# Another order of the same operations in the five instruction streams of a two-layer attention and convolution kernel

## The reference

```
y   = x + attention(group_norm(x))
out = y + conv(group_norm(y))
```

## Time and profile before

| what | value |
|---|---|
| median of 3 runs | 1963.32 us |
| profiled execution, time | 1962.26 us |
| profiled execution, span from first to last instruction | 1960.5 us |
| TensorE busy | 1861.5 us (95%) |
| VectorE busy | 1632.6 us (83%) |
| ScalarE busy | 1369.6 us (70%) |
| GpSimd busy | 1311.3 us (67%) |
| SyncE's DMA queue, share of the 16 DMA engines | 75.3% |
| mean granted TensorE clock | 0.989 |

### The profile page before, as it was taken

The page is one execution under the profiler, slowest core; times in us unless marked ns, Lnnn a source line. Parts: engine busy times, 40 slices in busy tenths (PEclk is TensorE's granted clock), DMA queues, the critical chain, the costliest instruction groups (busy, mean ns, idle before and its releaser), DMA issues.

```text
span 1960.5 us, 51383 instructions
## 1 busy us (share of the span) xinstructions
PE 1861.5 (95%) x21521; PEld 993.2 (51%) x21521; DVE 1632.6 (83%) x3108; ACT 1369.6 (70%) x1480; POOL 1311.3 (67%) x729
## 2 busy tenths in 40 slices
PE   3799999999999999999999999999999999999997
PEld 1455554555554555544555544555544555544552
DVE  6778888888888788888888888888888888888874
ACT  4677776776776777766777766777676777766761
POOL 6476767686666676767676767676667686667670
PEclk8989999999999999999999999999999999999999
DMA  6267877887877797877788878787877797877765
GB/s 130 46 139 157 178 165 155 169 176 160 171 164 161 150 180 157 178 164 159 162 181 152 178 162 157 163 181 150 180 160 161 157 182 156 177 165 157 156 145 145
DMA packets 349430, 313.01 MB, mean 160 GB/s; under 512 B 299152, under 2 KB 299920, under 8 KB 341008
## 3 DMA queue, kind: packets, MB, share of 16 engines
q1 hardware_dynamic: 346656, 305.75, 75.3%
q10 hardware_dynamic: 2224, 3.97, 0.8%
q0 software_dynamic: 320, 0.01, 0.0%
HBM read 68.10 MB, written 67.11 MB: 69 GB/s over the span
## 4 chain that ended last, share of the span: by engine, by line
PE 54%; SPq 21%; DVE 18%; DMA 4%; issue 2%; ACT 1%; POOL 0%; ACTq 0%; DVEq 0%; POOLq 0%
PE pair_ps L922 18%; PE pair_ps L904 8%; DVE km L1286 7%; SPq L334 6%; SPq L321 5%; PE pair_ps L913 5%; PE pair_ps L863 4%; SPq L333 4%; DVE u L1283 4%; DVE image L1338 4%; PE pair_ps L885 3%; PE bank_ps L814 3%; DMA replicas<-yg_lo 3%; PE pair_ps L823 3%; SPq L306 2%; SPq L327 2%
## 5 line engine op out<-in xcount | busy, mean ns | idle before, releaser
L922 PE MATMUL pair_ps<-replicas,w_rep 96*32 96x512 f16 x8192 | 490.3, 383 | 18.0 <-DMA replicas<-yg_lo 18.0
L489 POOL TENSOR_TENSOR u_lo<-u,u_hi 128x1024 f16<-128x1024 f32 x128 | 269.9, 2139 | 280.2 <-ACT u_hi L608 280.2
L492 POOL TENSOR_TENSOR exp_kT_lo<-exp_kT,exp_kT_hi 128x1024 f16<-128x1024 f32 x128 | 273.1, 2134 | 192.8 <-ACT exp_kT_hi L620 190.2
L922 PEld LDWEIGHTS pair_ps<-replicas,w_rep 96*32 96x32 f16 x8192 | 201.6, 96 | 279.8 <-issue 76.7
L495 POOL TENSOR_TENSOR u_lo<-exp_q,u_hi 128x1024 f16<-128x1024 f32 x128 | 270.4, 2142 | 25.7 <-ACT u_hi L626 25.2
L608 ACT ACTIVATE u_hi<-u 128x1024 f16<-128x1024 f32 x128 | 135.3, 1057 | 144.5 <-DVE u L1283 137.5
L1338 DVE SCALAR_TENSOR_TENSOR image<-pair_ps,image 128x512 f32<-128x512 f32 x256 | 175.5, 686 | 45.3 <-PE pair_ps L922 41.3
L626 ACT ACTIVATE u_hi<-exp_q 128x1024 f16<-128x1024 f32 x128 | 131.5, 1050 | 109.2 <-DVE exp_q L1325 109.0
L485 POOL TENSOR_SCALAR u<-image,st 128x1024 f32<-128x1024 f32 x128 | 179.3, 1409 | 29.4 <-DVE st L1222 29.4
L863 PE MATMUL pair_ps<-wqk_hi,u_hi 128*128 128x128 f16 x1024 | 181.5, 222 | 0.0
L1325 DVE TENSOR_TENSOR exp_q<-exp_q,pair_ps 128x1024 f32<-128x1024 f32 x128 | 152.9, 1216 | 32.8 <-PE pair_ps L823 29.8
(11 more groups left out here) (184 smaller groups left out, 4500.2 us busy)
## 6 DMA issues: line engine op xcount, KB each, us to landing
image<-in_x SPq DMA_DIRECT2D x256, 256.0 KB, 4.8
out<-image SPq DMA_DIRECT2D x502, 128.0 KB, 2.3
replicas<-yg_hi SPq DMA_DIRECT2D x252, 165.0 KB, 3.7
replicas<-yg_hi SPq DMA_DIRECT2D x252, 107.2 KB, 2.4
replicas<-yg_lo SPq DMA_DIRECT2D x126, 165.0 KB, 4.2
replicas<-yg_lo SPq DMA_DIRECT2D x126, 107.2 KB, 2.3
uT_hi<-u_hi SPq DMA_TRANSPOSE x128, 4.4
uT_lo<-u_lo SPq DMA_TRANSPOSE x128, 4.0
```

What stands on the lines that cost most here:

```text
L489: pool.tensor_tensor(px(UL, v), px(U, v), px(UH, v), ALU.subtract).then_inc(ul_ready, 1)
L492: pool.tensor_tensor(KL[:, v % 2], KT[:, v % 2], KH[:, v % 2], ALU.subtract).then_inc(kl_ready, 1)
L922: mm = pe.matmul(conv_ps[32 * r:32 * r + 32, j % 2], w_rep[0:32 * SLOTS, tap, r], rep[:, j * ROWS + dy:(j + 1) * ROWS + dy, dx:dx + SIDE], ...
```

## The change

No operation is added or taken away and none changes its size. Only the place in the stream, the PSUM tile of some, and the waits are changed:

- `inv_norm` 2 and 3, `normalise` 0 to 3, `rough_k` 0, `max_k` 0, `high_u` 0, `conv_dense` 6, `conv_ring` 5 and 6 and `finish` 5 and 6 move from the beginning of a step to the end of the step before.
- On VectorE `y_moments` goes between `row_k` and `max_q` 0, `y_seed` and `y_scale` between `max_q` 1 and 2, `low_y` 0 before `rows_q`, all `x_stats` behind `rows_q`; `keep_turned` goes behind two `soften`.
- On TensorE `context` 1 goes behind `queries` 1, `context` 2 and 3 behind `conv_dense` 0 and 1 (so directly ahead of `conv_ring` 0); `rough_q` 0 goes ahead of `turn_k_max`; the broadcasts and `norm_sums` are grouped.
- On SyncE the stores of units 0 and 1 move over the border between two steps (same place in the queue), `turn_u` 0 goes ahead of `store` 2, and `replicate_high` 0 goes ahead of `turn_u` 3.
- In `drain`, the work that moved is no longer there; ScalarE's queue gets the stores of units 0 and 1 of image 30.

Core of the diff (TensorE, then VectorE, then SyncE):

```diff
@@ tensor step @@
-                if e is not None:
-                    pe.wait_ge(out_ready, at(e, CHUNKS, 5))
-                    conv_dense(e, 6)
-                if a is not None:
-                    pe.wait_ge(u_ready, at(a, UNITS, 1))
-                    inv_norm(a, 2, pair_ps[0])
-                    pe.wait_ge(u_ready, at(a, UNITS, 2))
-                    inv_norm(a, 3, pair_ps[1])
...
+                    rough_k(a, 1, pair_ps[0])
                 if e is not None:
                     pe.wait_ge(out_ready, at(e, CHUNKS, 6))
                     conv_dense(e, 7)
+                if a is not None:
+                    pe.wait_ge(uh_ready, at(a, UNITS, 3))
+                    rough_k(a, 2, pair_ps[1])
+                    pe.wait_ge(k_max, at(a, 8, 2))
+                    pe.wait_ge(uh_ready, at(a, UNITS, 4))
+                    rough_k(a, 3, pair_ps[0])
+                if e is not None:
                     conv_ring(e, 7)
                 if a is not None:
+                    pe.wait_ge(k_max, at(a, 8, 3))
+                    rough_q(a, 0, pair_ps[1])
                     pe.wait_ge(k_max, at(a, 8, 7))
                     turn_k_max(bank_ps[1])
-                    rough_q(a, 0, pair_ps[1])
                     rough_q(a, 1, pair_ps[0])
...
                 if c is not None:
                     pe.wait_ge(lo_even, at(c, UNITS // 2, 1))
                     conv_dense(c, 0)
                     conv_dense(c, 1)
+                if a is not None:
+                    pe.wait_ge(uT_in[2], at(a, 32, 32))
+                    pe.wait_ge(kl_ready, at(a, UNITS, 3))
+                    context(a, 2, bank_ps[0])
+                    pe.wait_ge(uT_in[3], at(a, 32, 32))
+                    pe.wait_ge(kl_ready, at(a, UNITS, 4))
+                    context(a, 3, bank_ps[0])
...
+                if p is not None:
+                    pe.wait_ge(norm_dve, at(p, 5, 5))
+                    inv_norm(p, 0, pair_ps[0])
                 if c is not None:
                     conv_ring(c, 4)
                 if p is not None:
                     if a is not None:
                         pe.wait_ge(y_ready, at(a, UNITS, 4))
                     inv_norm(p, 1, pair_ps[1])
+                    pe.wait_ge(u_ready, at(p, UNITS, 1))
+                    inv_norm(p, 2, pair_ps[0])
+                if c is not None:
+                    conv_ring(c, 5)
+                if p is not None:
+                    pe.wait_ge(u_ready, at(p, UNITS, 2))
+                    inv_norm(p, 3, pair_ps[1])
+                if c is not None:
+                    pe.wait_ge(out_ready, at(c, CHUNKS, 5))
+                    conv_dense(c, 6)
+                if p is not None:
+                    pe.wait_ge(u_ready, at(p, UNITS, 3))
+                    pe.wait_ge(uh_ready, at(p, UNITS, 1))
+                    rough_k(p, 0, pair_ps[0])
+                if c is not None:
+                    conv_ring(c, 6)
@@ vector step @@
                 if a is not None:
                     dve.wait_ge(max_turned, at(a, 2, 1))
                     row_k(a, bank_ps[1])
+                if c is not None:
+                    dve.wait_ge(y_squared, at(c, UNITS, 4))
+                    y_moments(c)
+                if a is not None:
                     max_q(a, 0, pair_ps[1])
                     dve.wait_ge(q_rough, at(a, UNITS, 2))
                     max_q(a, 1, pair_ps[0])
+                if c is not None:
+                    dve.wait_ge(y_group, at(c, 1, 1))
+                    y_seed(c, bank_ps[0])
+                    dve.wait_ge(y_stat, at(c, Y_STEPS, 9))
+                    y_scale(c)
...
                     dve.wait_ge(q_rough, at(a, UNITS, 4))
-                    max_q(a, 3, pair_ps[1])
+                    max_q(a, 3, pair_ps[0])
+                if c is not None:
+                    dve.wait_ge(hi_ready, at(c, UNITS, 1))
+                    dve.wait_ge(yg_ready, at(c, UNITS, 1))
+                    low_y(c, 0)
+                if a is not None:
+                    dve.wait_ge(max_turned, at(a, 2, 2))
+                    rows_q(a, bank_ps[1])
...
+                    dve.wait_ge(k_rough, at(p, UNITS, 1))
+                    max_k(p, 0, pair_ps[0])
+                if c is not None:
+                    dve.wait_ge(conv_done, at(c, CHUNKS, 6))
+                    finish(c, 5)
+                    dve.wait_ge(conv_done, at(c, CHUNKS, 7))
+                    finish(c, 6)
@@ sync step @@
                 if a is not None:
                     sp.wait_ge(ul_ready, at(a, UNITS, 3))
                     turn_u(a, 2)
+                if c is not None:
+                    sp.wait_ge(hi_ready, at(c, UNITS, 2))
+                    replicate_high(c, 0)
+                if a is not None:
                     sp.wait_ge(ul_ready, at(a, UNITS, 4))
                     turn_u(a, 3)
                 if c is not None:
-                    sp.wait_ge(hi_ready, at(c, UNITS, 2))
-                    replicate_high(c, 0)
                     sp.wait_ge(lo_even, at(c, UNITS // 2, 1))
                     sp.wait_ge(lo_odd, at(c, UNITS // 2, 1))
                     replicate_low(c, 0)
```

More of the change, by code:

```diff
@@ L380, in step @@
                 if e is not None:
+                    sp.wait_ge(out_ready, at(e, CHUNKS, 6))
+                    store(e, 2)
                     sp.wait_ge(out_ready, at(e, CHUNKS, 8))
@@ L990, in step @@
                     rough_q(a, 2, pair_ps[1])
+                if c is not None:
+                    pe.wait_ge(y_stat, at(c, Y_STEPS, 4))
+                    group_means(1, bank_ps[0], y_group)
+                if a is not None:
                     pe.wait_ge(q_max, at(a, 5, 2))
@@ L993, in step @@
                     keys(a, 1, pair_ps[0])
-                if c is not None:
-                    pe.wait_ge(y_stat, at(c, Y_STEPS, 4))
-                    group_means(1, bank_ps[1], y_group)
-                if a is not None:
                     pe.wait_ge(kT_exp, at(a, UNITS, 1))
@@ L1010, in step @@
                     turn_q_max(bank_ps[1])
+                    pe.wait_ge(kT_exp, at(a, UNITS, 3))
+                    keys(a, 3, pair_ps[2])
+                    pe.wait_ge(q_max, at(a, 5, 5))
+                    queries(a, 0, pair_ps[1])
+                    queries(a, 1, pair_ps[0])
                     pe.wait_ge(kl_ready, at(a, UNITS, 2))
@@ L1025, in step @@
                 if a is not None:
-                    pe.wait_ge(kl_ready, at(a, UNITS, 3))
-                    pe.wait_ge(uT_in[2], at(a, 32, 32))
-                    context(a, 2, bank_ps[0])
+                    pe.wait_ge(q_exp, at(a, UNITS, 2))
+                    queries(a, 3, pair_ps[0])
                     if p is not None:
@@ L1400, in step @@
                     x_stats(p, 0)
-                if a is not None:
-                    dve.wait_ge(max_turned, at(a, 2, 2))
-                    rows_q(a, bank_ps[1])
-                if c is not None:
-                    dve.wait_ge(yg_ready, at(c, UNITS, 1))
-                    dve.wait_ge(hi_ready, at(c, UNITS, 1))
-                    low_y(c, 0)
-                if p is not None and not first(p):
                     x_stats(p, 1)
@@ L1416, in step @@
                     x_seed(p, bank_ps[1])
+                if c is not None:
+                    dve.wait_ge(yg_ready, at(c, UNITS, 3))
+                    dve.wait_ge(hi_ready, at(c, UNITS, 3))
+                    low_y(c, 2)
+                if p is not None and not first(p):
                     dve.wait_ge(x_stat, at(p, X_STEPS, 8))
                     x_scale(p)
-                if c is not None:
-                    dve.wait_ge(hi_ready, at(c, UNITS, 3))
-                    dve.wait_ge(yg_ready, at(c, UNITS, 3))
-                    low_y(c, 2)
                 if a is not None:
-                    dve.wait_ge(ctx_sum, at(a, UNITS, 4))
-                    weigh_context(a, bank_ps[0])
                     dve.wait_ge(den_act, at(a, 2, 2))
@@ L1472, in step @@
                     dve.wait_ge(mixed, at(a, UNITS, 4))
-                    residual(a, 3, pair_ps[0])
+                    residual(a, 3, pair_ps[1])
+                if p is not None:
+                    dve.wait_ge(inv_bcast, at(p, UNITS, 1))
+                    normalise(p, 0, pair_ps[0])
                 if c is not None:
@@ L1481, in drain @@
                 dve.wait_ge(y_group, at(c, 1, 1))
-                y_seed(c, bank_ps[1])
+                y_seed(c, bank_ps[0])
                 dve.wait_ge(y_stat, at(c, Y_STEPS, 9))
```

297 lines of the change are left out of this document (128 added, 169 removed).

## The result

The changed kernel takes 1972.8 us (median of 8 runs, 1965.8 to 1977.2), the kernel before 1963.8 us (8 runs): ratio 1.0053, 95% interval 1.0038 to 1.0069. The forecast was 1943 with a range of 1927 to 1968, so both the size and the sign were wrong. The profiled execution took 1970.8 us with a span of 1969.0.

What follows compares the result with a forecast made beforehand. TensorE's own stream was taken as the bound, with about 1.5 us of waits in 58.8. Profiled 1962.26 - 24.8 (31 steps, period 58.84 to 58.04) + 4.2 (end) = 1941.7; median 1.06 higher: 1943, range 1927 to 1968.

Steps and rivals of the forecast that it cites:

- Part 1: TensorE from `queries` 0 to the end of `conv_ring` 6: 46.30 us falls to 41.62, with no new waits.
- changes of kind: Switches between full, 32-row and 32-column products on TensorE, 0.11 us each: 27 before, 18 after, 0.99 us saved.
- 57.79: Forecast length in us of one round with nothing late: 41.62 on TensorE plus 16.17 on VectorE.
- Part 2: VectorE from the end of ring 6 to `rows_q` becomes the bound: 16.17 us, with TensorE waiting 1.5 in small pieces.
- Part 3: DMAs ahead of `conv_ring` 0: queue 7.9 us instead of 8.65, so most of the replicas' 16.7 us wait goes.
- leftover: Mean allowance for late transfers and the slower clock behind a long wait: 0.25 us a step, giving period 58.04.
- Part 4, the start: First steps, without convolution, hardly change in order: 0 us, bounds -2 and +2.
- Part 4, the end: Last image's y statistics wait for rings 5 and 6 and their `finish`: +4.2 us, bounds +1 and +6.
- a period of 58.4 or more: Sign named for the prediction being wrong: `turn_k_max` coming this many us apart, where 58.0 was expected.
- The transfers: Rival: transfers through the one queue stay as late, ring 0 waits 0.54 us a step: 1954 us, chance 0.18.
- `low_y` 0: Rival: this VectorE operation ahead of `rows_q` lengthens, at 2.57 us adding 0.72 a round: 1965 us, chance 0.12.
- `turn_u` 3: Slower rival: its transpose held behind the replicas delays `context` 3 and ring 0, up to 2009 us, chance 0.15.

Runs made afterwards that it cites:

- run 2: Changed kernel with `norm_sums` of units 0 and 1 together behind ring 1, units 2 and 3 together behind ring 2: 1942.63 us, ratio 0.9922 to the kernel before.
- run 3: Changed kernel with `conv_dense` 0 moved ahead of `group_means` and the denominators: 1969.06 us, ratio 1.0045 to the kernel before.
- run 9: Changed kernel with the two DMA transposes of unit 3 left out after the first image (computation incomplete): 1959.35 us, ratio 0.9966 to the kernel before.
- run 4: Changed kernel with the two PSUM tiles of the rough scores exchanged, `rough_k` 1 to `queries` 3: 1967.17 us, ratio 1.0043 to the kernel before.
- run 5: Changed kernel with the statistics of x ahead of `rows_q` in step 1 alone (unit 3 behind): 1971.92 us, ratio 1.0031 to the kernel before.
- run 6: Changed kernel with the last image's end put back into the order of before: 1973.48 us, ratio 1.0028 to the kernel before.
- run 10: Changed kernel with `norm_sums` in pairs, x statistics ahead of `rows_q` in step 1, and the old order of the end: 1944.28 us, ratio 0.9890.
- run 8: Changed kernel with `conv_dense` 0 ahead of the denominators and unit 3's two DMA transposes left out after the first image: 1946.28 us, ratio 0.9907.
- run 11: Changed kernel with `norm_sums` pairs, `conv_dense` 0 ahead of the denominators, step 1's x statistics ahead of `rows_q`, old order of the end: 1949.45 us, ratio 0.9916.
- run 1: Kernel before with `norm_sums` of unit 0 moved ahead of the broadcast of unit 0, away from unit 1's: 1986.35 us, ratio 1.0133.
- run 7: Changed kernel with unit 3's denominator broadcast moved from beside unit 2's to behind `norm_sums` 2, ahead of ring 2: 1997.94 us, ratio 1.0169.

## Why the prediction was wrong

- **Part 1, "this is right only if nothing new waits in it", and the assumption under it that a moved product costs what it cost before: failed.** This is the step that took the steady gain away. The count of changes of kind, 27 and 18, is right. The undisturbed round came out at 58.27, not 57.79. `norm_sums` in new places cost 0.84 more (run 2), the denominators' wait for `exp_queries` 3 0.41 (run 3; I had checked VectorE's order against TensorE and passed over ScalarE in a sentence). In the other direction the broadcasts now stand beside each other in three places, two taking 0.33 where one took 0.32; with the changes of kind already in the sum, 0.2 at each was not: -0.6 (read off rows, not tried alone). And VectorE's line was 0.09 shorter. 57.79 + 0.84 + 0.41 - 0.6 - 0.09 = 58.35, against 58.27. I took the kind of tile into account as a price for each change, and overlooked the other half: products on different tiles of one kind run together.
- **Part 2: right.** 16.08 for 16.17, and the waits stand where they were named, at 0.45, 0.18, 0.16 and, for `turn_q_max`, some 0.2, about 1 us where 1.5 was summed. Only `queries` 0 doesn't wait: it follows `keys` 3 at once, and `rows_q` ends 0.06 before it starts (1473.75).
- **Part 3: right in direction, too small a leftover.** The replicas' wait fell to 5.9 us in the profile, but late transfers cost 0.38 a step in all (run 9), not 0.25, and 0.2 to 0.6 in the profiles of runs 4 to 6. The wait itself was 4.6 to 11.4 us in the profiles of runs 4 to 6, which have the same steady order of operations.
- **Part 4, the start at "0, bounds -2 and +2": failed, 9.1 us.** It put the whole start at nothing because "the first steps have no convolution, so their order hardly changes", and had no term for the clock. Without convolution nothing covers a VectorE line that is reordered: `x_stats` went behind `rows_q` and the first image's weight work, `group_means` waited 3.8 us, and the clock was low for longer, 6.5 of the 8.7 us in steps 1 and 2 by the estimate of run 5. Run 5 brought 6.5 us of this back in its profile, but together with the pairs the same edit brought nothing (run 10): what ends a stretch at the low clock early or late there was not found.
- **Part 4, the end: +3.8 for +4.2, near by luck.** By the estimate of run 6 the order, which the sum had at 4.2, cost 2.5 us, and the clock, for which it had no term, 1.3. Putting the order back returned 1.2.
- **Rivals.** None of them was it, though a sign that the prediction named for being wrong, a period of 58.4 or more, came true for another reason. The transfers play the part given to them, but as the floor under any gain ahead of ring 0 (runs 3, 8, 9, 11). `low_y` 0 took 1.79, and `turn_u` 3 never held `context` 3 for more than 0.9 us.

## What to carry to other kernels

Before moving a matmul that writes only part of the array's columns or reads part of its rows, look at its neighbours on disjoint tiles: a moved product can cost its full length where it had cost nothing, and taking one pair apart cost 27 us here, 18 of them in the steady steps. A reordering has to be priced against every engine that releases into it, and in the first and last rounds too, where the usual cover is missing and a longer stretch at the low clock can cost more than the wait that came before it (6.5 and 2.1 us here, an estimate). When a step's shortest length falls and its average doesn't, look for the transfer that takes the difference back, and shorten the queue ahead of it before tuning the engine.

## What the runs showed of the hardware

- Two units of `norm_sums`, eight f32 products on four 32-column tiles, took 0.90 us next to each other and 0.86 for one unit alone, each without its change of kind (before, changed kernel and run 1). Products on different column tiles start together: the first four of the denominators before at 951.07 to 951.09. The neighbour needn't be of the same operation: `mix_weights` starts its first products 0.01 us behind one of `norm_sums` (1436.82 and 1436.83), and ring 2 has most of its products from 1438.36 on, while the last ones of `norm_sums` 2 run from 1438.16 to 1438.76. One 32-row broadcast put among them cost 0.57 beyond its own 0.31 (run 7).
- Two broadcasts on four 32-row tiles took 0.33 together and 0.31 to 0.32 one alone.
- The granted clock stayed low while TensorE was busy again: in the changed kernel it was 0.56 from 100 to 110 us (5.7 us of products) and 0.50 from 110 to 120 (9.2 us of products); before it was 0.50 (7.7 us of products), then 0.97 (10.0 us of products). In run 2 it was 0.56 (5.8 us), then 0.76 (9.3 us of products), so nearly the same busy time went with another clock; what decides it these runs don't show. The price of a thin start was thus more than its waits.
- A wait ahead of one unit of a pair takes about its own length from what the pair saves: the denominators of unit 3 came 0.4 us late, and the sixteen products took 2.26 us for 1.85 (run 3).
